# Moving the attention outputs of a head pair one slot back, from the end of a slot to between its two score halves

## The chip, the cores and the metric

The kernel runs on 1 core of a Trainium2 chip. The metric is the device time of one execution in microseconds (us); lower is better. The engines are named as the profile names them: PE (TensorE, matmul), PEld (its weight loads, which overlap PE), DVE (VectorE), ACT (ScalarE), POOL (GpSimd), SP (SyncE, which issues most DMAs). "PSUM" is the memory into which PE writes, in banks of 128 x 512 fp32; eight of them exist here and all eight have names.

## What is computed

A cross-attention layer (16 heads of 64, 256 tokens against 512 context rows, four batches) and after it a small second layer (attention between the 16 head groups of each token, then eight experts mixed by a gate). Cut to the part that the change touches:

```python
lat = layer_norm(latents); ctx = layer_norm(context)
q = (lat @ Wq).reshape(b, n, HEADS, DHEAD).transpose(0, 2, 1, 3)
k, v = jnp.split(ctx @ Wkv, 2, axis=-1)          # heads split in the same way
k = apply_rope(k, cos, sin)
attn = jnp.clip(jnp.einsum('bhnd,bhsd->bhns', q, k) * scale, -11.0, 11.0)
attn = jax.nn.softmax(attn, axis=-1)
out = jnp.einsum('bhns,bhsd->bhnd', attn, v)     # "outputs" of a pair: pv
x = x + (out.transpose(0, 2, 1, 3).reshape(b, n, INNER) @ Wo + bo)
# then the second layer on x (rms norm, q/k/v, att over heads, Wo, gate, 8 experts)
```

## The kernel before

**Slots.** The 16 heads make 8 pairs, and four batches make 32 pairs. Every engine has its own program, written out by hand as a loop over slots from -3 to 32; slot s is about pair s. Order on one engine is fixed by this code, and engines meet through semaphores only. An engine whose next instruction waits does nothing else in the meantime.

**PE in slot s** (lines 739 to 756): the key projection of pair s+3 (`keys`, L517 to L519 on `ctxT,wkA`), the first half of the scores of pair s (`scores`, L579, 12 matmuls), a side step "a", the query projection of pair s+1 (`queries`, L517 to L519 on `latT,wqS`), in even slots the softmax denominators of two pairs (`sums`, L609), the second half of the scores, none to two units of the value projection (`values`, on `wvS`), a side step "b", the outputs of pair s-1 (`times_values`, L593, 16 matmuls in the trace), a side step "c".

**The score loop.** Both halves of the scores go into the same two banks, `sc`. So each half waits for ACT's exponential of the half before it (`s_exp`, lines 572 and 573), which in turn waits for the scores (L805) and writes `e`. POOL then clips `e` (L1515), and `sums` and `times_values` wait for both clips of their pair. `e` has three buffers: the exponential of pair j waits for the outputs of pair j-3 (L807). ACT copies the outputs out of their bank, `pv`, in `attention_copy` (L817).

**Side steps.** What the second layer needs of PE, and the transposes of the next batch, lies in the slots by the tables `POST_STEPS` and `PREP_STEPS` under the places a, b and c. Inside the slots all of them write one and the same bank, `side`, and each waits until the step before it has been read out of the bank by DVE or ACT (line 638, `s_side_free`). In these slots both b and c hold a step:

| slots | step b, who reads it out | step c |
|---|---|---|
| 9, 17, 25 | `norm1`, DVE (L1124) | `norm2` |
| 11, 19 | `ctx_T`, ACT (L839) | `h_T` |
| 18, 26 | `out_proj`, DVE (L1129) | `o_T` |
| 20, 28 | `keyval2`, DVE (L1143) | `h2_T` |
| 22, 30 | `moe0`, ACT (L884, four pieces) | `moe1` |

No other slot has steps at both b and c. `times_values` stood between the two.

**Cover at the end of a slot.** Behind the second half of the scores, slots 5, 8, 13, 16, 21, 24 and 29 hold no values and no side step, only the outputs and the next keys; from slot 29 on there are no next keys either, since pair 32 does not exist.

**DVE in a slot** multiplies the keys by cosine and sine (L1075), splits off the low parts of queries and keys (L1011) and does the work of the second layer on fixed places (`OWN_STEPS`). The value and key projections use two banks, `pj_k`, in turn; each waits until the last use of its bank has been read out by DVE or ACT (`bank_free`). At the end of a batch DVE takes the reciprocals of the sums (L1087) and splits them (`recS`), and `norm0` on PE waits for these.

Of the kernel before, what the change touches and what calls it, by code (L numbers as in the profile page):

```python
# [42 lines left out]
NPAIR = NB * PAIRS  # L43
# [134 lines left out]
def value_units(slot):  # L178


    b, p = divmod(slot, PAIRS)
    if p >= PAIRS - 2 and b + 1 < NB:
        first = 8 * (b + 1) + 2 * (p - (PAIRS - 2))
        return [first, first + 1]
    if 1 <= p <= 4 and 0 <= b < NB:
        return [8 * b + 3 + p]
    return []
# [25 lines left out]
def xattn_ffn(nc, x, ctx, cos, sin, ln_lat_g, ln_lat_b, ln_ctx_g, ln_ctx_b, Wq, Wkv, Wo, bo,  # L213
              gamma1, f_Wq, f_bq, f_Wdown, f_bdown, f_Wup, f_bup, f_Wo, f_bo, gamma2, f_Wg, f_bg, f_We, out):
    es = ExitStack()
    with es:
# [220 lines left out]
        def taken(name, b):  # L437

            k, n = SIDE[name, b]
            return s_side_free[k], n + 1  # L440
# [7 lines left out]
        def query_bank(j):  # L448
            return pj_k[PLACE["queries", j] % 2]
# [64 lines left out]
        def _(pe):  # L514
            def split3(out_ap, w_hi, w_lo, m_hi, m_lo):

                nc.tensor.matmul(out_ap, w_hi, m_hi, start=True, stop=False)  # L517
                nc.tensor.matmul(out_ap, w_hi, m_lo, start=False, stop=False)  # L518
                return nc.tensor.matmul(out_ap, w_lo, m_hi, start=False, stop=True)  # L519

            def bank_free(kind, n):
                if PLACE[kind, n] < 2:
                    return
                kind, n = PROJECTIONS[PLACE[kind, n] - 2]
                if kind == "keys":
                    pe.wait_ge(s_kmul, 2 * n + 2)
                elif kind == "queries":
                    pe.wait_ge(s_qlo, n + 1)
                else:
                    pe.wait_ge(s_v, n + 1)  # L530

            def keys(j):
                b, p = divmod(j, PAIRS)
                cols = slice(128 * p, 128 * p + 128)
                if p == 0:
                    pe.wait_ge(s_ctxT, b + 1)
                if j == 0:
                    pe.wait_ge(s_wk, 1)
                bank_free("keys", j)
                split3(key_bank(j)[:, :], wkA[:, 0, cols], wkA[:, 1, cols], ctxT[:, b % 2, 0, :],  # L540
                       ctxT[:, b % 2, 1, :]).then_inc(s_kproj, 1)

            def queries(j):
                b, p = divmod(j, PAIRS)
                if p == 0:
                    pe.wait_ge(s_latT, b + 1)
                if j == 0:
                    pe.wait_ge(s_wq, 1)
                bank_free("queries", j)
                cols = slice(128 * p, 128 * p + 128)  # L550
                split3(query_bank(j)[:, 0:NT], wqS[:, 0, cols], wqS[:, 1, cols], latT[:, 0, :], latT[:, 1, :]).then_inc(s_qproj, 1)

            def values(n):
                b, unit = divmod(n, 8)
                half, c = divmod(unit, SC)
                if n == 0:
                    pe.wait_ge(s_wv, 1)
                if not value_units_at_first(n):
                    bank_free("values", n)
                rows = slice(128 * c, 128 * c + 128)  # L560
                cols = slice(512 * half, 512 * half + 512)
                split3(value_bank(n)[:, :], ctxT[:, b % 2, 0, rows], ctxT[:, b % 2, 1, rows], wvS[:, 0, cols], wvS[:, 1, cols])\
                    .then_inc(s_vproj, 1)

            def scores(j, half):

                if half == 0:
                    pe.wait_ge(s_klo, j + 1)
                    pe.wait_ge(s_qlo, j + 1)
                if j == 0 and half == 0:  # L570
                    pe.wait_ge(s_v, 2)
                if j or half:
                    pe.wait_ge(s_exp, 2 * j + half)
                for c in range(2):
                    chunk = slice(128 * (2 * half + c), 128 * (2 * half + c) + 128)
                    for k_part, q_part in ((0, 0), (0, 1), (1, 0)):
                        for h in range(2):
                            rows = slice(DH * h, DH * h + DH)
                            last = nc.tensor.matmul(sc[:, h, c * NT:(c + 1) * NT], ks[rows, j % 3, k_part, chunk],  # L579
                                                    qs[rows, j % 2, q_part, :], start=(k_part + q_part == 0),  # L580
                                                    stop=(k_part == 1))
                last.then_inc(s_score, 1)
# [14 lines left out]
            def sums(j):  # L597

                b, p = divmod(j, PAIRS)
                pe.wait_ge(s_clip, 2 * j + 2)  # L600
                if p == 1 and b:
                    pe.wait_ge(s_rec, b)
                if j == 1:
                    pe.wait_ge(s_const, 2)
                    pe.wait_ge(s_v, 4)
                w = sum_rows[:, 24 - 8 * (p // 2):56 - 8 * (p // 2)]
                for c in range(SC):
                    for g in range(4):
                        last = nc.tensor.matmul(sum_bank[32 * g:32 * g + 32, 0:NT], w,  # L609
                                                e[:, (j - 1 + g // 2) % 3, g % 2, c, :],  # L610
                                                start=(p == 1 and c == 0), stop=(p == PAIRS - 1 and c == SC - 1))
                last.then_inc(s_sum, 1)
# [116 lines left out]
            def side_at(slot, pos):  # L729
                step = side_step(slot, pos)  # L730
                if step:
                    side_product(*step)
# [6 lines left out]
            for slot in range(-KEYS_AHEAD, AFTER):  # L739
                if slot + KEYS_AHEAD < NPAIR:  # L740
                    keys(slot + KEYS_AHEAD)
                if 0 <= slot < NPAIR:
                    scores(slot, 0)
                side_at(slot, "a")
                if 0 <= slot + 1 < NPAIR:
                    queries(slot + 1)
                if 2 <= slot <= NPAIR and slot % 2 == 0:
                    sums(slot - 1)
                if 0 <= slot < NPAIR:
                    scores(slot, 1)  # L750
                for n in value_units(slot):
                    values(n)
                side_at(slot, "b")
                if 1 <= slot <= NPAIR:
                    times_values(slot - 1)
                side_at(slot, "c")
            for name, b, k in TAIL_STEPS:
# [11 lines left out]
        def _(act):  # L769
# [18 lines left out]
            def query_hi(j):  # L788
                act.wait_ge(s_qproj, j + 1)
                if j >= 2:  # L790
                    act.wait_ge(s_score, 2 * (j - 2) + 2)
                nc.scalar.activation(qs[:, j % 2, 0, :], query_bank(j)[:, 0:NT], ACT.Copy).then_inc(s_qhi, 1)  # L792
# [10 lines left out]
            def exps(j, half):  # L803

                act.wait_ge(s_score, 2 * j + half + 1)  # L805
                if j >= 3 and half == 0:
                    act.wait_ge(s_pv, j - 2)  # L807
                    act.wait_ge(s_sum, (j - 1) // 2)
                nc.scalar.activation(e[:, j % 3, :, 2 * half:2 * half + 2, :].rearrange("p h c n -> p h (c n)"),  # L809
                                     sc[:, :, :], ACT.Exp, scale=SCALE).then_inc(s_exp, 1)  # L810

            def attention_copy(j):
                act.wait_ge(s_pv, j + 1)
                if j >= PAIRS:

                    act.wait_ge(*taken(f"norm{j % PAIRS // 2}", j // PAIRS - 1))
                nc.scalar.activation(u[:, j % PAIRS, :], pv_bank[:, 0:NT], ACT.Copy).then_inc(s_u, 1)  # L817
# [119 lines left out]
            for slot in range(-KEYS_AHEAD, AFTER):  # L937
                if 0 <= slot < NPAIR:
                    exps(slot, 0)
                side_taken(slot, "a")  # L940
                if 0 <= slot + 1 < NPAIR:
                    query_hi(slot + 1)
                if 0 <= slot < NPAIR:
                    exps(slot, 1)
                for n in value_units(slot):
                    value_copy(n)
                if 0 <= slot + KV_AHEAD < NPAIR:
                    key_hi(slot + KV_AHEAD)
                side_taken(slot, "b")
                if 1 <= slot <= NPAIR:  # L950
                    attention_copy(slot - 1)
                second_layer(slot, "c")
                side_taken(slot, "c")
                second_layer(slot, "end")
                gate_exps(slot)
                if slot == PAIRS - 2:
                    order_columns()
# [684 lines left out]
```

## Time and profile before

| what | value |
|---|---|
| time, median of 3 runs | 344.45 us (344.03 to 344.72) |
| the profiled execution | 343.19 us |
| its span, first to last instruction | 340.3 us |
| granted PE clock, mean | 0.97 of full speed |
| PE busy | 307.5 us (90%) |
| DVE busy | 246.0 us (72%) |
| POOL busy | 202.3 us (59%) |
| ACT busy | 156.5 us (46%) |
| scores L579 busy, 64 halves | 63.5 us |
| outputs L593 busy, 32 pairs | 62.3 us |
| sums L609 busy, 16 times | 30.9 us |

The page gives shares of the whole span. The idle time of PE is spread over a start, a tail and single short waits inside the slots, so the views to read are the table of who waited for whom and the timeline, slot by slot. The start of a matmul group minus the start of the group before it tells how much of PE's time that group took; the durations printed for pipelined matmuls overlap a little, and are not to be added.

### The profile page before, as it was taken

How to read it: one execution, taken by the hardware profiler on the slowest of the kernel's cores; microseconds unless marked ns; L12 is line 12 of the kernel's file. 1: busy time of each engine (PE TensorE's matmuls, PEld its weight loads, DVE VectorE, ACT ScalarE, POOL GpSimd, SP SyncE). 2: the span in 40 equal slices, each digit the busy share in tenths (PEclk: the TensorE clock that was granted, in tenths of full speed). 3: DMA queues.
4: the chain of work that ended last, by engine and by line, in shares of the span. 5: the costliest groups of instructions: out<-in, count | busy, mean ns of one | idle time of the engine just before them, and what ended most of it. 6: DMA issues, size and time to landing. Idle time of an engine off the chain costs nothing.

```text
span 340.3 us, 6782 instructions
## 1 busy us (share of the span) xinstructions
PE 307.5 (90%) x2584; PEld 211.5 (62%) x2584; DVE 246.0 (72%) x470; ACT 156.5 (46%) x291; POOL 202.3 (59%) x206
## 2 busy tenths in 40 slices
PE   6858999999999999997999999997999999889674
PEld 5736666666667666665686666665866645769351
DVE  3956734433893658999938789797375987799977
ACT  2445564566533636644336467753354465020420
POOL 5426654534564659495547593898275937855661
PEclk9797999999999999999999999999999999979985
DMA  8843222111210101101201110111111000000001
GB/s 218 231 134 82 53 47 64 32 33 42 50 34 2 44 22 47 25 24 40 56 0 33 31 41 23 33 34 31 33 31 49 2 0 3 15 2 0 1 0 31
DMA packets 16320, 14.24 MB, mean 42 GB/s; under 512 B 4833, under 2 KB 11809, under 8 KB 16289
## 3 DMA queue, kind: packets, MB, share of 16 engines
q1 hardware_dynamic: 15232, 13.69, 15.4%
q8 instruction: 20, 0.33, 0.4%
q10 hardware_dynamic: 1056, 0.13, 0.2%
q14 instruction: 12, 0.09, 0.1%
HBM read 4.89 MB, written 0.52 MB: 16 GB/s over the span
## 4 chain that ended last, share of the span: by engine, by line
PE 58%; DVE 25%; ACT 7%; POOL 3%; issue 3%; DMA 2%; SPq 0%; ACTq 0%; DVEq 0%; POOLq 0%
PE sc L579 13%; PE pv L593 13%; PE sums L609 7%; PE pj_k L517 5%; ACT e L809 4%; DVE o L1326 3%; PE pj_k L519 3%; PE pj_k L518 3%; PE side L680 3%; DVE ks L1011 2%; PE side L726 2%; PE side L616 2%; DMA sin_in<-in_L_xattn_sin_dram 2%; DVE rec L1087 2%; POOL prod L986 1%
## 5 line engine op out<-in xcount | busy, mean ns | idle before, releaser
L1515 POOL TENSOR_SCALAR e<-e 128x1024 f32<-128x1024 f32 x64 | 68.4, 1069 | 75.6 <-ACT e L809 66.1
L809 ACT ACTIVATE e<-sc 128x1024 f32<-128x1024 f32 x64 | 65.7, 1027 | 76.5 <-PE sc L579 76.5
L579 PE MATMUL sc<-qs,ks 64*128 64x256 f32 x768 | 63.5, 298 | 6.1 <-ACT e L809 4.5
L579 PEld LDWEIGHTS sc<-qs,ks 64*128 64x128 f32 x768 | 50.4, 188 | 28.3 <-issue 17.3
L593 PE MATMUL pv<-e,v 128*64 128x256 f32 x512 | 62.3, 385 | 0.0
L1508 POOL TENSOR_TENSOR krot<-kcos,kswap 128x512 f32<-128x512 f32 x32 | 41.2, 1286 | 11.7 <-DMA kswap<-ksin 9.5
L593 PEld LDWEIGHTS pv<-e,v 128*64 128x64 f32 x512 | 33.9, 136 | 22.4 <-issue 5.6
L1075 DVE TENSOR_TENSOR ksin<-pj_k,sinT 128x512 f32<-128x512 f32 x32 | 22.0, 688 | 34.4 <-PE pj_k L519 30.7
L1011 DVE TENSOR_TENSOR ks<-krot,ks 128x512 fp32r<-128x512 f32 x32 | 33.0, 1030 | 0.0
L609 PE MATMUL sums<-e,sum_rows 128*32 128x256 f32 x512 | 30.9, 382 | 1.0 <-POOL e L1515 1.0
L817 ACT ACTIVATE u<-pv 128x256 f32<-128x256 f32 x32 | 12.3, 385 | 37.7 <-PE pv L593 37.7
L986 POOL TENSOR_TENSOR prod<-q,kv 128x1024 f32<-128x1024 f32 x8 | 19.9, 2496 | 5.6 <-DVE kv L1206 3.5
L1011 DVE TENSOR_TENSOR qs<-pj_k,qs 128x256 fp32r<-128x256 f32 x32 | 13.4, 420 | 13.0 <-ACT qs L792 12.9
L994 POOL TENSOR_TENSOR prod<-att,kv 128x1024 f32<-128x1024 f32 x8 | 19.1, 2398 | 5.9 <-ACT att L903 5.5
L609 PEld LDWEIGHTS sums<-e,sum_rows 128*32 128x32 f32 x512 | 15.0, 109 | 12.1 <-POOL e L1515 2.0
L786 ACT ACTIVATE ks<-krot 128x512 fp32r<-128x512 f32 x32 | 20.1, 627 | 4.9 <-POOL krot L1508 4.9
L1075 DVE TENSOR_TENSOR kcos<-pj_k,cosT 128x512 f32<-128x512 f32 x32 | 21.7, 678 | 0.0
L1326 DVE TENSOR_REDUCE o<-prod 128x64 f32<-128x1024 f32 x16 | 18.8, 1207 | 0.1
L801 ACT ACTIVATE v<-pj_k 128x512 f32<-128x512 f32 x28 | 16.6, 594 | 4.2 <-PE pj_k L519 3.7
L517 PE MATMUL pj_k<-ctxT,wkA 128*128 128x512 f32 x32 | 15.7, 491 | 2.9 <-DVE kcos L1075 2.8
L517 PE MATMUL pj_k<-wvS,ctxT 128*128 128x512 f32 x28 | 13.4, 480 | 3.8 <-DVE kcos L1075 3.8
L1557 POOL TENSOR_TENSOR moe<-moe 128x512 f32<-128x512 f32 (+2 forms) x18 | 15.4, 854 | 1.2
(265 smaller groups left out, 558.9 us busy)
## 6 DMA issues: line engine op xcount, KB each, us to landing
kswap<-ksin SPq DMA_DIRECT2D x128, 64.0 KB, 2.0
ctx_in<-in_ctx_dram SPq DMA_DIRECT2D x4, 256.0 KB, 3.1
prod<-in_L_xattn_Wkv_dram SPq DMA_DIRECT2D x2, 512.0 KB, 6.5
x_in<-in_x_dram SPq DMA_DIRECT2D x1, 512.0 KB, 6.2
prod<-in_L_xattn_Wq_dram SPq DMA_DIRECT2D x1, 512.0 KB, 7.0
wo<-in_L_xattn_Wo_dram SPq DMA_DIRECT2D x1, 512.0 KB, 8.0
fwe<-in_L_ffn_We_dram SPq DMA_DIRECT2D x1, 512.0 KB, 4.0
out_dram<-x_in SPq DMA_DIRECT2D x3, 128.0 KB, 1.8
```

The source lines that it names most:

```text
L517: nc.tensor.matmul(out_ap, w_hi, m_hi, start=True, stop=False)
L579: last = nc.tensor.matmul(sc[:, h, c * NT:(c + 1) * NT], ks[rows, j % 3, k_part, chunk], qs[rows, j % 2, q_part, :], start=(k_part + q_par ...
L593: last = nc.tensor.matmul(pv_bank[DH * h:DH * h + DH, 0:NT], v[:, c, col:col + DH], e[:, j % 3, h, c, :], start=(c == 0), stop=(c == SC - 1))
L609: last = nc.tensor.matmul(sum_bank[32 * g:32 * g + 32, 0:NT], w, e[:, (j - 1 + g // 2) % 3, g % 2, c, :], start=(p == 1 and c == 0), stop= ...
L786: nc.scalar.activation(ks[:, j % 3, 0, :], krot[:, j % 2, :], ACT.Copy).then_inc(s_khi, 1)
L809: nc.scalar.activation(e[:, j % 3, :, 2 * half:2 * half + 2, :].rearrange("p h c n -> p h (c n)"), sc[:, :, :], ACT.Exp, scale=SCALE).then ...
L986: return engine.tensor_tensor(prod[:, t, 1024 * hh:1024 * hh + 1024].rearrange("p (h g d) -> p h g d", h=G // 2, g=G), q_v.unsqueeze(2).to ...
L1011: return nc.vector.tensor_tensor(dst, whole, f(hi), ALU.subtract)
L1075: nc.vector.tensor_tensor(dst[:, j % 2, :], key_bank(j)[:, :], trig[:, :], ALU.mult).then_inc(s_kmul, 1)
L1326: return nc.vector.tensor_reduce(outputs(t)[:, 8 * hh:8 * hh + 8, :], pr, AX, ALU.add)
L1508: nc.gpsimd.tensor_tensor(krot[:, j % 2, :], kcos[:, j % 2, :], kswap[:, j % 2, :], ALU.add)\
L1515: nc.gpsimd.tensor_scalar(a, a, EXP_HIGH, EXP_LOW, ALU.min, ALU.max).then_inc(s_clip, 1)
```

## The change

`times_values` and `attention_copy` take other places in their engines' loops. For slots 2 to 31, PE now runs the outputs of pair s-2 (before: pair s-1) between the queries and the sums, thus between the two score halves, and ACT copies them out ahead of its second exponential. Slot 31 also runs the outputs of pair 30 at the old place, and slot 32 those of pair 31. No instruction is added or removed; side steps, buffers and waits are as they were.

```diff
 (PE)
                 if 0 <= slot + 1 < NPAIR:
                     queries(slot + 1)
+
+                if 2 <= slot < NPAIR:
+                    times_values(slot - 2)
                 if 2 <= slot <= NPAIR and slot % 2 == 0:
                     sums(slot - 1)
...
                 side_at(slot, "b")
-                if 1 <= slot <= NPAIR:
+                if NPAIR - 1 <= slot <= NPAIR:
                     times_values(slot - 1)
 (ACT)
+                if 2 <= slot < NPAIR:
+                    attention_copy(slot - 2)
                 if 0 <= slot < NPAIR:
                     exps(slot, 1)
...
-                if 1 <= slot <= NPAIR:
+                if NPAIR - 1 <= slot <= NPAIR:
                     attention_copy(slot - 1)
```

PE in slot 5 and at the start of slot 6, before (the first L579 is the first half of slot 5, `ctxT,wkA` are keys, `latT,wqS` queries, `pv<-e,v` outputs):

```order
L579 MATMUL sc<-qs,ks 128x256 x12
L517 MATMUL pj_k<-latT,wqS 128x256
L518 MATMUL pj_k<-latT,wqS 128x256
L519 MATMUL pj_k<-latT,wqS 128x256
L579 MATMUL sc<-qs,ks 128x256 x12
L593 MATMUL pv<-e,v 64x256 x8
L517 MATMUL pj_k<-ctxT,wkA 128x512
L518 MATMUL pj_k<-ctxT,wkA 128x512
L519 MATMUL pj_k<-ctxT,wkA 128x512
L579 MATMUL sc<-qs,ks 128x256 x12
```

The same stretch of PE's program with the change:

```order
L579 MATMUL sc<-qs,ks 128x256 x12
L517 MATMUL pj_k<-latT,wqS 128x256
L518 MATMUL pj_k<-latT,wqS 128x256
L519 MATMUL pj_k<-latT,wqS 128x256
L593 MATMUL pv<-e,v 64x256 x8
L579 MATMUL sc<-qs,ks 128x256 x12
L517 MATMUL pj_k<-ctxT,wkA 128x512
L518 MATMUL pj_k<-ctxT,wkA 128x512
L519 MATMUL pj_k<-ctxT,wkA 128x512
L579 MATMUL sc<-qs,ks 128x256 x12
```

The outputs have moved in front of the second score half, and only the keys are left behind it.

PE at the end of slot 11, as a piece of the difference (`ident,ctx_n` is `ctx_T`, step b; `ident,hn` is `h_T`, step c; both write the bank `side`):

```order
 L519 MATMUL pj_k0<-wvS,ctxT 128x512
 L616 MATMUL side<-ident,ctx_n 128x128 x4
-L593 MATMUL pv<-e,v 64x256 x8
 L616 MATMUL side<-ident,hn 128x128 x2
 L517 MATMUL pj_k1<-ctxT,wkA 128x512
```

The two users of the bank `side` now stand directly one behind the other, as in the other ten slots of the table above.

ACT in slot 22, before (`moe<-side,gate` reads `moe0` and then `moe1` out of the bank `side`; `u<-pv` is the copy of outputs, `e<-sc` the exponential):

```order
L809 ACTIVATE e<-sc 128x2x512
L801 ACTIVATE v<-pj_k 128x512 x2
L786 ACTIVATE ks<-krot 128x512
L884 ACTIVATE moe<-side,gate 128x128 x4
L817 ACTIVATE u<-pv 128x256
L884 ACTIVATE moe<-side,gate 128x128 x4
```

With the change (three lines were added above, so L809 is L812 and so on):

```order
L820 ACTIVATE u<-pv 128x256
L812 ACTIVATE e<-sc 128x2x512
L804 ACTIVATE v<-pj_k 128x512 x2
L789 ACTIVATE ks<-krot 128x512
L887 ACTIVATE moe<-side,gate 128x128 x8
```

The copy now stands ahead of the second exponential, and the two read-outs of `side` follow each other.

## Rows read from the trace of the kernel before

**Rows 1.** Waits of PE over the span: total us, times, longest.
```profile
PE pj_k L517 <- DVE kcos L1075: 6.9, 4, 2.8
PE sc L579 <- ACT e L809: 4.5, 9, 0.6
PE sums L609 <- POOL e L1515: 1.0, 1, 1.0
PE side L671 <- DVE recS L1011: 0.6, 1, 0.6
```
**Rows 2.** Timeline of PE, slots 5 and 6: start, us, engine, line, op.
```profile
60.55 0.98 PE L579 MATMUL sc<-qs,ks 64*128 64x256 f32 x12
...
62.65 0.98 PE L579 MATMUL sc<-qs,ks 64*128 64x256 f32 x12 [0.57 <-ACT e L809]
63.55 1.95 PE L593 MATMUL pv<-e,v 128*64 128x256 f32 x16
65.43 0.50 PE L517 MATMUL pj_k<-ctxT,wkA 128*128 128x512 f32 x1
...
66.33 0.98 PE L579 MATMUL sc<-qs,ks 64*128 64x256 f32 x12
```
**Rows 3.** Chain that ended last, in order of time: one step, between them.
```profile
61.57 1.03 ACT e L809
```
**Rows 4.** Timeline of PE, slot 19: end of the queries, second score half.
```profile
178.90 0.28 PE L519 MATMUL pj_k<-latT,wqS 128*128 128x256 f32 x1
179.30 0.98 PE L579 MATMUL sc<-qs,ks 64*128 64x256 f32 x12
```
**Rows 5.** Timeline of PE and DVE, slot 9: behind norm1.
```profile
93.82 1.95 PE L593 MATMUL pv<-e,v 128*64 128x256 f32 x16
...
94.00 0.69 DVE L1124 TENSOR_TENSOR on<-u,side 128x512 f32<-128x512 f32 x1 [0.82 <-PE side L672]
```
**Rows 6.** Timeline of PE and DVE, slot 18: behind out_proj.
```profile
174.26 1.95 PE L593 MATMUL pv<-e,v 128*64 128x256 f32 x16
...
174.44 0.42 DVE L1129 TENSOR_TENSOR x_in<-side,x_in 128x256 f32<-128x256 f32 x1 [3.57 <-PE side L680]
```
**Rows 7.** Timeline of PE and DVE, slot 20: behind keyval2.
```profile
192.02 1.95 PE L593 MATMUL pv<-e,v 128*64 128x256 f32 x16
...
192.20 0.69 DVE L1143 TENSOR_TENSOR kv<-side,fbkv 128x512 f32<-128x512 f32 x1 [2.06 <-PE side L706]
```
**Rows 8.** Timeline of PE and ACT, slot 11: behind ctx_T.
```profile
113.35 1.95 PE L593 MATMUL pv<-e,v 128*64 128x256 f32 x16
...
114.04 0.78 ACT L839 ACTIVATE ctxT_f<-side,vec 128x512 f32<-128x512 f32 x1
```
**Rows 9.** Timeline of PE and ACT, slot 22: behind moe0.
```profile
207.58 1.95 PE L593 MATMUL pv<-e,v 128*64 128x256 f32 x16
...
207.84 1.14 ACT L884 ACTIVATE moe<-side,gate 128x128 f32<-128x128 f32 x4
```
**Rows 10.** Timeline of DVE: last waits before its two full stretches, and recS.
```profile
128.82 0.42 DVE L1011 TENSOR_TENSOR qs<-pj_k,qs 128x256 fp32r<-128x256 f32 x1 [0.55 <-ACT qs L792]
135.46 0.42 DVE L1011 TENSOR_TENSOR qs<-pj_k,qs 128x256 fp32r<-128x256 f32 x1 [0.91 <-ACT qs L792]
...
155.55 0.42 DVE L1011 TENSOR_TENSOR recS<-rec,recS 128x256 fp32r<-128x256 f32 x1
...
214.74 0.42 DVE L1011 TENSOR_TENSOR qs<-pj_k,qs 128x256 fp32r<-128x256 f32 x1 [2.06 <-ACT qs L792]
```
**Rows 11.** Timeline of PE where those two stretches end, slots 17 and 25.
```profile
160.50 0.50 PE L517 MATMUL pj_k<-wvS,ctxT 128*128 128x512 f32 x1 [2.04 <-DVE kcos L1075]
...
232.09 0.50 PE L517 MATMUL pj_k<-wvS,ctxT 128*128 128x512 f32 x1 [1.77 <-DVE kcos L1075]
```
**Rows 12.** Busy time by stretch (PE, PEld, DVE, ACT, POOL, then PEclk, DMA).
```profile
228.00:234.00 6.00, 3.88 (x32) 3.15 (x34) 5.97 (x10) 3.12 (x5) 5.68 (x7) 1.00 0.11 28
```
**Rows 13.** Timeline of PE, slot 30: sums.
```profile
272.67 1.93 PE L609 MATMUL sums<-e,sum_rows 128*32 128x256 f32 x32 [1.00 <-POOL e L1515]
```

## The prediction

> **What bounds the kernel now.** I read the waits of PE first, then its timeline slot by slot, then the timelines of DVE, ACT and POOL at the places where PE waits. PE is the busiest engine, and inside the slots it waits little: for exponentials, for DVE's key products, once for POOL's clip, once for the reciprocals [rows 1]. So the time of the slots is nearly PE's own work, and the change can gain no more than these waits, while each new hole in PE's row is paid at once. The exception is two stretches in which DVE never waits, from 135.5 to 160.4 and from 214.7 to 232.0 us [rows 10]; at the end of each PE waits for DVE [rows 11]. There DVE sets the time, and PE has 2.04 and 1.77 us to spare.
>
> The score loop has a floor. From one score half to the next at least 2.10 us pass (60.55 to 62.65), since the exponential runs from 61.57 to 62.60 and PE goes on 0.05 us later [rows 2, 3]. PE's work between two halves is free of waits only if half plus work last 2.10 us.
>
> **What the change removes: the waits between the halves.** In slot 5 PE has only the queries there and idles 0.57 us; a group normally starts 0.07 us before the printed end of the one before (63.55 + 1.95 = 65.50 against 65.43), so the hole is 0.64 us [rows 2]. The outputs take 1.88 us (63.55 to 65.43 [rows 2]) and now fill it. Slots 3, 5, 7, 11, 13 and 15 are alike: 6 x 0.64 = 3.8 us. In slots 9, 17, 19, 21, 27 and 29 a side step fills most of the hole; the rest is 179.30 - 178.90 - 0.28 + 0.07 = 0.19 us [rows 4], six times 1.1 us. In slot 30 the sums wait 1.00 us for POOL's clip [rows 13], and the outputs now stand in front of them: 1.0 us. In slot 31, where the outputs of pair 29 fill the hole, I take 0.2 us by the same row [rows 4]. Sum: 6.1 us. ACT's copy ahead of the second exponential costs nothing: ACT waits there for the second score half anyway, which PE runs after those outputs.
>
> **What it adds, first: short ends of slots.** Behind the second score half slot 5 now has the keys alone. From 62.65 to 66.33 PE took 3.68 us; without the outputs 1.80, and the floor is 2.10 [rows 2]: 0.30 us lost. Slots 5, 8, 13, 16, 21 and 24 are so: 1.8 us. In slot 29 there are no keys either: one half of 0.90 us (3.68 - 1.88 - 0.90, the keys being 65.43 to 66.33 [rows 2]) against 2.10, 1.2 us lost. Sum: 3.0 us.
>
> **Second: the bank `side`.** In eleven slots the outputs stood between steps b and c, and these share one bank, so c may start only when b has been read out. The outputs hid that. Now c comes to the head of PE's queue when the outputs used to start, and waits for the reader's end plus 0.05 us [rows 3]. Behind it in PE's queue stand the next keys and the next scores, so the whole slot moves.
> - `norm2` behind `norm1`: DVE reads 94.00 to 94.69, PE could go on at 93.82: 0.92 us [rows 5]; slots 9, 17, 25: 2.8 us.
> - `o_T` behind `out_proj`: 174.86 + 0.05 - 174.26 = 0.65 us [rows 6], slots 18, 26: 1.3 us.
> - `h2_T` behind `keyval2`: 192.89 + 0.05 - 192.02 = 0.92 us [rows 7], slots 20, 28: 1.8 us.
> - `h_T` behind `ctx_T`: ACT comes to it late, behind an exponential, a value copy and a key copy, 114.82 + 0.05 - 113.35 = 1.52 us [rows 8], slots 11, 19: 3.0 us.
> - `moe1` behind `moe0`: four pieces on ACT, 208.98 + 0.05 - 207.58 = 1.45 us [rows 9], slots 22, 30: 2.9 us.
>
> Sum: 11.8 us. The reading engine's place in its own order is the same behind the second score half, so the lag carries over. The bounds: nothing, if the read-out were long over when PE arrives, which rows 5 to 9 contradict, and 1.88 us each, the whole cover.
>
> The Trainium skill, "Perfetto Trace Analysis", section Optimizing Tensor Performance, Matmuls, says that independent matmul groups should rotate through different PSUM banks, so that one is read out while the next runs. By that rule this change is the wrong way round: two groups of one bank come to stand together. The rows show the mechanism and its size, and the sum above goes by them alone.
>
> **Third: DVE's stretches.** On PE alone the balance would be 11.8 + 3.0 - 6.1 = +8.7 us. But part of it falls where DVE sets the time, so I go through in order.
> - Up to slot 12: lost 0.30 (slot 8), 0.30 (slot 5), 0.92, 1.52; gained four times 0.64 (3, 5, 7, 11) and 0.19 (9). Balance +0.3 us.
> - First stretch. DVE waited 0.55 and 0.91 us for query copies just before it [rows 10]. Queries now reach ACT earlier than DVE wants them, as the outputs no longer stand ahead of keys and queries at a slot's start, so these 1.46 us go. DVE ends 1.46 - 0.3 = 1.1 us earlier than before, and PE, which had 2.04 us to spare, follows: -1.1 us at the values of slot 17. One new wait lies inside: `norm0` of slot 17 needs `recS`, ready at 155.97 before [rows 10], and PE now arrives about 0.9 us ahead of it; that fits into what is left of the 2.04 us.
> - Slots 17 to 23: +0.92, +0.65, +1.52 - 0.19, +0.92, -0.19 + 0.30, +1.45 = +5.4: balance +4.3 us. DVE's second stretch starts from a query copy [rows 10] which is now issued 1.88 us earlier within the slots: +2.4 us. It ends +2.4 us late. PE's own path would be there at +4.2 and still had 1.77 us to spare [rows 11], so both meet at +2.4 us.
> - From slot 25 on: +0.92, +0.65 - 0.19, +0.92, -0.19 + 1.2, -1.0, +1.45, -0.2 = +3.6: balance +6.0 us.
>
> Behind slot 31 nothing changes place: DVE waits for the last sums, and the tail starts later by all of it. The clock gives no further term: in a stretch with a PE wait of 1.77 us it was granted in full [rows 12], and the new waits are shorter. (On this, the Trainium skill, "TensorE: Matmul & The Clock Gate", section HAM oscillation, holds that waits between bursts can put the clock down by half; by it the eleven new holes might cost more, and the rows show no such fall.)
>
> So the profiled execution of 343.19 us (span 340.3) would become 349.2 us. It was 1.3 us quicker than the median of the runs, 344.45 us; on that the forecast is **350.4 us**, 1.7% slower.
>
> **The rivals.**
> - *DVE hides nothing.* If DVE's stretches begin later than I say (its waits before them stay, and `recS` comes late because the sums now stand 1.88 us later in slots 8, 16 and 24), PE's balance of 8.7 us stands in full, and some 1 us more if `norm0` waits in slots 9 and 25 as well: 353 to 354 us. For it: the rows show the sparing only at two places. Against: those are 3.8 us of real idle time of PE.
> - *The bank waits are half.* If ACT and DVE, relieved of the outputs' copy at the slot's end and of waiting for it, reach the read-outs sooner, the 11.8 us become some 6, and the time is +6.0 - 5.9 = 344.5 us: no change. Only the five slots read by ACT have a queue that could shrink; DVE sat waiting in rows 5 to 7, so it has nothing to gain.
> - *Faster.* The copy of the outputs is gone from ACT's row at the end of a slot, and queries and keys reach DVE 1.88 us earlier within each slot; if by that step b is read out before PE comes to c in all eleven slots, no bank wait is left, and what remains is 344.45 + 3.0 - 6.1 = 341.4 us. It decides at bank waits of about 5.8 us in all, half a microsecond each, below which the change gains; rows 5 to 9 all stand above that.
> - *The change does not do what it says*: the order of PE in slots 5 and 11 shows that it does, and I give it nothing.
>
> **How the numbers follow.** Forecast (348 to 352) 0.65, DVE hides nothing (352 to 355) 0.17, half the bank waits (343.8 to 348) 0.12, faster 0.06. The range, 346.5 to 353.8, leaves some 0.1 out below and 0.07 above. A difference of 0.2%, 0.7 us, is about what a measurement of this kernel can tell from none: slower takes the forecast, the first rival and half of the second (0.88), same most of the rest of the second (0.05), faster the third and a hundredth of the second (0.07).
>
> **What would show each step.** In the trace of the changed kernel the waits of the scores for the exponential should vanish between the halves and come back at 0.2 to 0.3 us at the ends of slots 5, 8, 13, 16, 21, 24, and at 1.1 us in slot 29. PE should wait for DVE's L1124, L1129 and L1143 (the lines of before; all three are three lines further down now) 0.6 to 0.9 us seven times, and for ACT's read-outs of `ctx_T` and `moe0` 1.4 us four times. The wait for key products in slot 17 should fall from 2.0 to about 0.5 us, and the one in slot 25 to nearly nothing. The prediction is wrong if the waits on `side` sum to less than 6 us, or if the two waits for key products keep their size while the rest comes as said.

## The result, and the profile after

| | before | after |
|---|---|---|
| time, median | 344.24 us (342.98 to 344.72, 4 runs) | 351.75 us (351.48 to 352.14, 4 runs) |
| ratio, 95% interval | | 1.0216 [1.0173, 1.0258] |
| profiled execution, its span | 343.19, 340.3 us | 351.48, 349.7 us |
| granted PE clock, mean | 0.970 | 0.966 |

The change makes the kernel 2.2% slower, 7.5 us between the medians. The forecast was 350.4 us, 6.0 us over the 344.45 us that were known when it was made; the range, 346.5 to 353.8, held the time.

The page of the changed kernel: its span, the busy time of the engines, and the groups of the score loop with DVE's key split (count | busy us, mean ns of one | idle before them and what ended it):
```profile
span 349.7 us, 6782 instructions
...
PE 307.7 (88%) x2584; PEld 211.9 (61%) x2584; DVE 251.8 (72%) x470; ACT 156.4 (45%) x291; POOL 202.5 (58%) x206
...
L579 PE MATMUL sc<-qs,ks 64*128 64x256 f32 x768 | 63.8, 299 | 4.7 <-ACT e L812 3.5
L593 PE MATMUL pv<-e,v 128*64 128x256 f32 x512 | 62.3, 385 | 0.0
L1016 DVE TENSOR_TENSOR ks<-krot,ks 128x512 fp32r<-128x512 f32 x32 | 35.8, 1119 | 0.0
```
PE is as busy as before (307.7 against 307.5 us) in a span 9.4 us longer: the added time is waiting. Who makes it wait stands in the waits of PE in the changed kernel, cut to the score loop, from the second half of the scores of slot 1 (32.65 us) to that of slot 31 (290.28). Columns as in [rows 1]: total us, times, longest:
```profile
PE side L671 <- DVE on L1129: 3.1, 3, 1.4
PE side L726 <- ACT moe L887: 3.0, 3, 1.4
PE sc L579 <- ACT e L812: 3.0, 6, 1.2
PE side L616 <- ACT ctxT_f L842: 2.9, 2, 1.5
PE side L671 <- DVE recS L1016: 2.1, 2, 1.6
PE side L616 <- DVE kv L1148: 1.7, 2, 0.9
PE side L616 <- DVE x_in L1134: 1.2, 2, 0.6
PE pj_k L517 <- DVE kcos L1080: 1.1, 3, 0.6
PE sc L579 <- DVE ks L1016: 1.1, 1, 1.1
```
Five of these rows, on `side` for `on`, `moe`, `ctxT_f`, `kv` and `x_in`, are steps c that wait for the read-out of their step b. They sum to 11.9 us; 0.3 us of it, a third wait for `moe` (slot 31), was there before. The wait of the sums for POOL [rows 1, 13] is gone.

PE's timeline in slot 5 of the changed kernel (start, us, engine, line) shows both sides of the move, and answers [rows 2]:
```profile
58.25 1.95 PE L593 MATMUL pv<-e,v 128*64 128x256 f32 x16
60.12 0.97 PE L579 MATMUL sc<-qs,ks 64*128 64x256 f32 x12
...
62.30 0.98 PE L579 MATMUL sc<-qs,ks 64*128 64x256 f32 x12 [0.31 <-ACT e L812]
```
The second half of the scores (60.12) follows the outputs without a wait, where 0.57 us stood before. At the slot's end only the keys are left, and the next scores wait 0.31 us. Slot 11, PE and then ACT, answers [rows 8]:
```profile
111.08 0.60 PE L616 MATMUL side<-ident,ctx_n 128*128 128x128 f32 x4
113.13 0.44 PE L616 MATMUL side<-ident,hn 128*128 128x128 f32 x2 [1.45 <-ACT ctxT_f L842]
```
```profile
111.30 0.59 ACT L804 ACTIVATE v<-pj_k 128x512 f32<-128x512 f32 x1
111.78 0.63 ACT L789 ACTIVATE ks<-krot 128x512 fp32r<-128x512 f32 x1
112.30 0.78 ACT L842 ACTIVATE ctxT_f<-side,vec 128x512 f32<-128x512 f32 x1
```
`ctx_T` leaves PE at about 111.6; ACT comes to its read-out at 112.30, behind a value copy and a key copy, and ends it at 113.08. `h_T` starts 0.05 us later. All of it was predicted; 1.45 against 1.52 us is a matter of counting, since the view takes a wait from the printed end of the group before (111.08 + 0.60 = 111.68) and the forecast from 0.07 us earlier.

### The profile page after: what moved, and what is told of

It reads as the page before. It is cut to its first block, busy times and chain, and to the rows that moved or that the text cites. A ratio compares the mean times of both kernels' runs of the same rounds, so it can differ in the third digit from the quotient of the medians.

```text
span 349.7 us, 6782 instructions
## 1 busy us (share of the span) xinstructions
PE 307.7 (88%) x2584; PEld 211.9 (61%) x2584; DVE 251.8 (72%) x470; ACT 156.4 (45%) x291; POOL 202.5 (58%) x206
## 4 chain that ended last, share of the span: by engine, by line
PE 58%; DVE 28%; ACT 5%; issue 5%; DMA 2%; POOL 1%; SPq 0%; DVEq 0%; ACTq 0%; POOLq 0%
PE pv L593 13%; PE sc L579 12%; PE sums L609 7%; PE pj_k L517 5%; PE side L680 3%; PE pj_k L519 3%; PE pj_k L518 3%; DVE ks L1016 3%; DVE o L1331 2%; PE side L726 2%; ACT e L812 2%; ACT moe L887 2%; DVE ksin L1080 2%; DVE rec L1092 1%; DVE kcos L1080 1%
## 5 line engine op out<-in xcount | busy, mean ns | idle before, releaser
L1520 POOL TENSOR_SCALAR e<-e 128x1024 f32<-128x1024 f32 x64 | 69.1, 1079 | 85.6 <-ACT e L812 81.3
L812 ACT ACTIVATE e<-sc 128x1024 f32<-128x1024 f32 x64 | 65.6, 1026 | 71.8 <-PE sc L579 71.8
L579 PEld LDWEIGHTS sc<-qs,ks 64*128 64x128 f32 x768 | 50.7, 189 | 29.5 <-issue 24.0
L579 PE MATMUL sc<-qs,ks 64*128 64x256 f32 x768 | 63.8, 299 | 4.7 <-ACT e L812 3.5
L1016 DVE TENSOR_TENSOR ks<-krot,ks 128x512 fp32r<-128x512 f32 x32 | 35.8, 1119 | 0.0
L991 POOL TENSOR_TENSOR prod<-q,kv 128x1024 f32<-128x1024 f32 x8 | 19.6, 2454 | 6.4 <-DVE kv L1211 4.3
L1016 DVE TENSOR_TENSOR qs<-pj_k,qs 128x256 fp32r<-128x256 f32 x32 | 13.4, 418 | 11.8 <-ACT qs L795 11.7
```

The costliest lines, as they stand in the source:

```text
L991: return engine.tensor_tensor(prod[:, t, 1024 * hh:1024 * hh + 1024].rearrange("p (h g d) -> p h g d", h=G // 2, g=G), q_v.unsqueeze(2).to ...
L1016: return nc.vector.tensor_tensor(dst, whole, f(hi), ALU.subtract)
L1520: nc.gpsimd.tensor_scalar(a, a, EXP_HIGH, EXP_LOW, ALU.min, ALU.max).then_inc(s_clip, 1)
```

## The experiments

The spans differ by more than the loop does, since start and tail of this program vary by a microsecond: the changed kernel, run a second time, gave a loop of 257.69 us where it had 257.63, while its tail was 58.05 us where it had been 59.42. So beside the ratios, each of which is to the kernel before as it ran in the same row of runs, I compare the loop, scores of slot 1 to scores of slot 31 as above, and the waits that the view lists inside it. The column of the exponential also has the wait just ahead of the loop's first scores (0.56 us in the first two rows, 0.24 in the last):

| kernel | loop | on the bank of step c | exponential | key split `ks` | `recS` | `kcos` | other | all listed |
|---|---|---|---|---|---|---|---|---|
| before | 248.9 | 0.3 | 4.0 | - | 0.6 | 3.8 | 1.0 | 9.7 |
| after | 257.6 | 11.9 | 3.0 | 1.1 | 2.1 | 1.1 | 0.4 | 19.6 |
| outputs late in the eleven slots | 250.6 | 0.3 | 3.9 | - | 2.1 | 4.6 | 0.4 | 11.3 |
| step c behind the next keys | 256.6 | 6.3 | 3.0 | 1.8 | 2.1 | 1.1 | 1.5 | 15.8 |
| step c in another bank | 247.4 | 1.1 | 1.8 | 3.5 | 2.2 | 1.1 | 0.8 | 10.5 |
| bank and places | 247.3 | 1.1 | 1.0 | 3.1 | 1.6 | 1.1 | 0.5 | 8.4 |
| bank, places and product | 244.4 | 1.1 | 0.9 | 1.8 | 1.6 | 1.1 | 0.4 | 6.8 |

From before to after the listed waits grow by 9.9 us and the loop by 8.8; the difference is the six holes of 0.19 us [rows 4], 1.1 us, which are too short to be listed. Three of the loops hold something more that no wait shows: PE's granted clock fell to half for some 3 us (outputs late: from about 160.5 to 163.5 us; step c behind the next keys: 270 to 273; bank and places: 200 to 203), which took about 1.6 us of each. In the loops of the other four it stood at full speed.

My theory: the bank waits cost the time. Rivals: the lag of a slot in itself; the new place between the halves in any slot; the order against the sums; the copy ahead of the exponential. Unless it is said otherwise, edits are made on the changed kernel.

**Where the outputs stand.** Three kernels take the outputs of pair s-2 between the halves in some slots, and put them back between steps b and c in the others:
```diff
-                if 2 <= slot < NPAIR:
+                if 2 <= slot < NPAIR and between(slot):
                     times_values(slot - 2)
...
                 side_at(slot, "b")
+                if 2 <= slot < NPAIR and not between(slot):
+                    times_values(slot - 2)
```
(ACT's copy likewise.) In the first `between` is false in the eleven slots that hold both b and c, in the second it is true in those alone, in the third it is always false, which leaves the lag by itself.

> The changed kernel, but in the eleven slots with side steps at both b and c (9, 11, 17 to 20, 22, 25, 26, 28, 30) the outputs of pair s-2 and their copy stand between b and c again. Theory S (the bank side): the changed kernel's PE waits there, 3.1 + 1.2 + 1.7 for DVE and 2.9 + 2.7 for ACT, 11.6 us, go; the holes between the score halves that the outputs filled in these slots come back (0.64 in slot 11, 0.2 in five others, the sums' wait for the clip in slot 30, 1.0), some 2.6 us: 351.75 - 11.6 + 2.6 = 342.8 us, or up to 345 where DVE is in the lead. Rival D (the loss comes from DVE's two full stretches and from the outputs being one slot late, which stays here): 349 to 352.

> The opposite half: outputs of pair s-2 everywhere, but between the score halves only in the eleven slots with side steps at both b and c, and at the end of the slot in all others. Theory S: 11.6 us of waits against 2.6 us of holes filled, less what DVE's stretches hide (up to 3.8): 344.2 + 9 - 3.8 to + 0 = 349.5 to 353. Rival D: most of the moves are undone, so 344 to 346.

> Outputs of pair s-2 and their copy at the old place, at the end of the slot, in every slot: the one-slot lag alone. Theory S: neither the holes nor the side waits are touched, 344.2 within 1 us. Rival D: the lag itself moves DVE's and POOL's work against each other and costs several us: 347 or more.

Measured: with the outputs late in the eleven slots 344.35 us, ratio to before 1.0000 [0.9967, 1.0032]; between the halves in the eleven alone 351.68 us, 1.0228 [1.0158, 1.0299]; the lag alone 343.88 us, 0.9992 [0.9953, 1.0032]. The whole loss sits in the eleven slots, and neither the lag nor the place between the halves costs anything in the other nineteen. It gains nothing there either: five of the six large holes are filled, 3.2 us, but the short ends of seven slots give them back, and DVE makes PE wait longer, `kcos` 4.6 against 3.8 us and `recS` 2.1 against 0.6 in the table. (The loops of the other two kernels hold one group of outputs fewer than these and are not compared.) PE's waits in slot 17 of the first of these kernels, at `norm0` and at the values, and the outputs behind them:
```profile
154.48 0.36 PE L675 MATMUL side<-recS,spread 128*128 128x256 f32 x1 [1.57 <-DVE recS L1024]
...
158.85 0.50 PE L521 MATMUL pj_k<-wvS,ctxT 128*128 128x512 f32 x1 [2.41 <-DVE kcos L1088]
...
160.22 3.47 PE L597 MATMUL pv<-e,v 128*64 128x256 f32 x16
```
PE waits 1.57 + 2.41 us for DVE within five microseconds, where it had waited 2.04 [rows 11]. The outputs behind take 3.40 us up to the next group (163.62) and not 1.88: the granted clock was 0.74 from 160 to 161 us and 0.50 from 161 to 163. So of the 1.7 us by which this loop is longer than that of before, 1.6 are the clock.

**Step c in another bank.** The sharper test keeps the place between the halves in all slots and takes away only what makes c wait. Step c of the eleven slots writes `pv`, which is free there, since its outputs were copied out in the middle of the slot; the next outputs wait until c has been read out:
```diff
+C_SLOT = {side_step(slot, "c"): slot for slot in range(NPAIR) if side_step(slot, "b") and side_step(slot, "c")}
...
+    in_slots = {step: 6 for step in C_SLOT}
...
+                read_out = sum(slot < j + 2 for slot in C_SLOT.values())
+                if read_out:
+                    pe.wait_ge(s_side_free[6], read_out)
...
+                elif (name, b) in C_SLOT:
+                    pe.wait_ge(s_u, C_SLOT[name, b] - 1)
```

> The changed kernel; in the eleven slots with side steps at both b and c, step c writes the bank of the outputs (pv), which is free there since the outputs of pair s-2 were copied out before, and no longer the bank side. Theory S: all eleven waits (11.6 us in the changed kernel's profile) go and the filled holes stay; where DVE is in the lead some of it is not seen: 351.75 - 11.6 = 340.2 us at best, 343 if DVE's stretches end as in the changed kernel. Rival D (the outputs between the halves cost by what they do to DVE and POOL, the bank is a symptom): 347 or more.

Measured: 342.64 us, 0.9964 [0.9934, 0.9995], and a loop 10.2 us shorter than that of the changed kernel. This shows the cause. Slot 11 on PE, where 1.45 us stood between the two steps:
```profile
112.33 0.60 PE L624 MATMUL side<-ident,ctx_n 128*128 128x128 f32 x4
112.77 0.38 PE L624 MATMUL pv<-ident,hn 128*128 128x128 f32 x2
```
The price of using `pv` is small: the read-out of `norm2` now holds up the outputs of slots 10 and 18, 1.1 us in all. DVE's key split has become the largest wait in the loop (3.5 us). Without its bank waits the move is no loss, and by a third of a per cent a gain, whose interval ends at 0.9995.

**Step c behind the next keys.** Keys of 0.90 us put between b and c should cover half of each bank wait:
```diff
                     keys(slot + KEYS_AHEAD)
+                side_at(slot - 1, "c")
                 if 0 <= slot < NPAIR:
                     scores(slot, 0)
```

> The changed kernel with one thing more: PE runs side step c behind the next slot's keys (0.90 us of work) and not ahead of them. Theory S: each wait on side shrinks by 0.90, so those behind norm1, out_proj and keyval2 go or stay under 0.5 us, those behind ctx_T and moe0 (slot 22) fall to about 0.5, and slot 30, which has no keys behind it, keeps its 1.3: about 8.5 us less than the changed kernel, 343 to 345 us. Rival D: PE's order there does not matter, 350 to 352.

Measured: 350.66 us, 1.0198 [1.0140, 1.0257], a miss: hardly better than the change itself, and inside what the rival had. The waits of the loop fall by 3.8 us, the loop by 1.0. Three rows of its PE timeline (slots 10, 22, and the keys behind slot 27) show where cover went, and a fourth (slot 29) where time went without a wait:
```profile
95.83 0.39 PE L671 MATMUL side<-recS,spread 128*128 128x256 f32 x1 [0.78 <-DVE on L1130]
...
202.50 0.97 PE L579 MATMUL sc<-qs,ks 64*128 64x256 f32 x12 [1.78 <-DVE ks L1017]
...
256.77 0.50 PE L517 MATMUL pj_k<-ctxT,wkA 128*128 128x512 f32 x1 [0.73 <-DVE qs L1017]
...
270.89 3.06 PE L593 MATMUL pv<-e,v 128*64 128x256 f32 x16
```
Step c moves 0.90 us nearer to step a of the next slot, and in slots 10 and 18 that one (`norm3`) waits on the same bank instead (0.78 and 0.79 us). The first scores of slot 22 wait 1.78 us for DVE where they waited 1.12, and the keys behind slot 27 wait for DVE's part of the queries in their bank. From slot 29 on there are no keys, so the steps c of slots 28 and 30 keep their waits of 0.85 and 1.31. With one bank in the row b, c, next a, the cover given to one pair was taken from the next in those slots. Of the 2.8 us of this loop that no listed wait shows, 1.6 us are the clock: it was granted at 0.50 from 270 to 273 us, and slot 29 took 5.39 us from its first to its second scores where the changed kernel took 3.79. The other 1.2 us are open. So the clock hides part of what the later place gives, but even without it the loop would be 2.6 us shorter and not 8.5.

**The order against the sums.** `sums` ahead of `times_values(slot - 2)`.

> The changed kernel with the sums ahead of the outputs in even slots. The sums then end 1.88 us earlier, as before the change. If the waits of norm0 for the reciprocals (2.1 us in two slots) and DVE's 1.0 us wait for the sums in slot 24 come from the outputs standing ahead of the sums, they go, and the sums of slot 30 wait for POOL's clip again (1.0 us): 350 to 351 us. If DVE's own queue sets them, nothing but the 1.0 us changes: 351.7 to 352.8.

Measured: 354.12 us, 1.0287 [1.0227, 1.0347], above both expectations, the loop 0.8 us longer than the changed kernel's. The waits of `norm0` in slots 9 (0.38) and 25 (0.52) do vanish, as the rival in the prediction had it, that in slot 17 only falls from 1.58 to 1.24, but the sums then wait for POOL's clip 2.3 us in all:
```profile
134.20 1.07 PE L609 MATMUL sums<-e,sum_rows 128*32 128x256 f32 x16 [1.48 <-POOL e L1520]
```
So in the loop the outputs ahead of the sums are the better order, and it was no cause of the loss.

**ACT's copy.** `attention_copy(slot - 2)` back at its old place behind step b.

> The changed kernel with ACT's copy of the outputs back behind the second exponential, at its old place behind step b. The prediction held that the copy ahead of the exponential costs nothing: 351.75 within 0.7 us, and by the same reasoning the late copy costs nothing either. If ACT's copy delays the exponential on which the next scores wait (0.08 us more at each short end), this comes out 0.5 us faster.

Measured: 354.69 us, 1.0296 [1.0245, 1.0346], 2.2 us above the expectation; the loop is the same as the changed kernel's to 0.1 us, and each of the short ends in slots 5, 8, 13 and 24 still takes 2.18 or 2.19 us, so the copy is not what makes them longer than 2.10. One new wait stands behind it, before the last outputs, since the copy of pair 29 now comes behind the last exponential:
```profile
294.83 1.95 PE L593 MATMUL pv<-e,v 128*64 128x256 f32 x16 [1.49 <-ACT u L820]
```
The copy ahead of the exponential costs nothing in the loop, as predicted, and saves 1.5 us at its end; the rest of the longer time is open.

**The product beside the key split.** In the changed kernel the first scores of slot 22 wait 1.12 us for `ks`, a wait that before did not have. DVE and POOL of the changed kernel in slot 21, each in order of time:
```profile
201.11 2.73 DVE L1016 TENSOR_TENSOR ks<-krot,ks 128x512 fp32r<-128x512 f32 x1
203.76 2.34 DVE L1178 TENSOR_REDUCE own_bank<-prod 128x128 f32<-128x1024 f32 x2
```
```profile
199.78 1.04 POOL L1520 TENSOR_SCALAR e<-e 128x1024 f32<-128x1024 f32 x1
200.91 2.38 POOL L991 TENSOR_TENSOR prod<-q,kv 128x1024 f32<-128x1024 f32 x1
```
The split is an instruction of 0.68 us that takes 2.73 here, and ends at 203.84, 0.55 us behind POOL's product (203.29). To test it, the product goes half a slot later:
```diff
-    "products_1b": [(5, 0)],
+    "products_1b": [(5, 1)],
```

> The changed kernel with POOL's second product of the second layer (products_1b) behind the clip of the second half and not ahead of it, in slots 13, 21 and 29. If DVE's key split of 2.73 us in slot 21 (0.7 alone) is slowed by POOL's product beside it, it falls below 1.4 us, the scores of slot 22 no longer wait 1.1 us for it, and the time is 350 to 351 us. If the split is slow for another reason, 351.7 within 0.7.

Measured: 353.13 us, 1.0272 [1.0209, 1.0334], no gain by the ratio and 2.1 us above what the theory had; but in the trace the loop is 0.9 us shorter and the wait for `ks` is gone. DVE and POOL there:
```profile
202.28 0.68 DVE L1016 TENSOR_TENSOR ks<-krot,ks 128x512 fp32r<-128x512 f32 x1
```
```profile
200.96 1.04 POOL L1520 TENSOR_SCALAR e<-e 128x1024 f32<-128x1024 f32 x1
204.17 1.04 POOL L1520 TENSOR_SCALAR e<-e 128x1024 f32<-128x1024 f32 x1 [2.17 <-DMA kswap<-ksin]
```
With nothing of POOL beside it the split takes 0.68 us. The mechanism is shown; that it moves the time of this kernel is not shown by this run.

**The three together.** Step c in `pv`, and the outputs at the slot's end in slots 8, 16, 21, 24 and 29, so that those ends do not run short; with the product at its place and with the product moved. The changed kernel ran again beside them.

> The same without POOL's product moved. Theory (prices add): the 2.0 us wait for DVE's key split of 2.7 us may stay in slot 22 or change with the place of the outputs in slot 21: 338.5 to 341. Rival (DVE hides it): 341 to 342.6, and then no difference from the run with the product moved.

> Step c of the eleven slots in the bank pv (as in the run before), POOL's second product behind the second clip, and the outputs at the end of the slot in slots 8, 16, 21, 24 and 29, where they leave the next scores to wait for the exponential. Theory: each price seen so far is its own and they add: against the run with the bank alone (342.6 us), 0.3 us less at each of slots 8, 16, 24 and 21, 1.0 less in slot 29, 0.4 to 0.6 less at norm0 of slots 9 and 25 since the sums end earlier, and the 2.0 us wait of slot 22's scores for DVE's key split falls to the 0.3 us of the exponential: 337.5 to 339.5 us, 1.5% faster than before. Rival: DVE is in the lead by now and hides it: 341 to 342.6.

> The changed kernel itself, on the chip of the two kernels beside it. 351.8 us and 1.022 of before if chips do not differ; the three variants of it that were run on another chip came out at 1.027 to 1.030, and if that is the chip and not the edits, it may show here or not. Its slots, from the second score half of slot 1 to that of slot 31, should take 257.6 us as in its first profile.

Measured: without the product's move 341.27 us, 0.9906 [0.9871, 0.9941]; with it 338.78 us, 0.9849 [0.9807, 0.9891], faster than both kernels. The changed kernel again: 351.46 us, 1.0213 [1.0162, 1.0263]. It repeats the first result. The three edits above stand at 1.027 to 1.030, though their loops differ from the changed kernel's by less than 1 us; whether that is the edits or the row of runs in which they ran is open. The chip, which the expectation suspects, was the same one in both rows of runs. The time without the product's move lies 0.3 us above what was expected and within what its rival gave (341 to 342.6), but the rival also had no difference between the two, and there is one: 2.5 us between the medians, though the intervals just overlap. The scores of slot 22, and then DVE's key split, with all three:
```profile
198.09 0.98 PE L588 MATMUL sc<-qs,ks 64*128 64x256 f32 x12 [0.51 <-DVE ks L1034]
```
```profile
196.66 1.38 DVE L1034 TENSOR_TENSOR ks<-krot,ks 128x512 fp32r<-128x512 f32 x1
```
and without the product's move (with the outputs that follow):
```profile
199.37 1.13 PE L588 MATMUL sc<-qs,ks 64*128 64x256 f32 x12 [1.83 <-DVE ks L1034]
...
201.69 2.79 PE L605 MATMUL pv<-e,v 128*64 128x256 f32 x16
```
```profile
196.62 2.69 DVE L1034 TENSOR_TENSOR ks<-krot,ks 128x512 fp32r<-128x512 f32 x1
```
The split starts at the same time in both and lasts 1.3 us less; PE waits 1.3 us less. The loops differ by 2.9 us, and 1.5 us of the rest is the clock again: without the product's move it was granted at 0.50 from 200 to 203 us, behind the wait of 1.83 us, and slot 22 took 6.91 us between its scores and not 5.37. Over its twelve executions the five with a mean clock of 0.974 or more took 338.35 to 340.82 us, the seven with 0.965 or less 341.12 to 342.73. So a part of the difference between the medians is the clock, and whether the longer wait brings that fall about is not shown: in the kernel with the other bank alone PE waits 2.04 us at the same place, and the clock stayed full.

## Why the prediction was right, and where it was not

**Holes between the halves: right.** They are gone in all slots named, with the wait of the sums in slot 30.

**Short ends of slots: right, 0.08 us too small each.** The floor was taken as 2.10 us and is 2.18 (60.12 to 62.30 above): 0.38 to 0.40 instead of 0.30 us in slots 5, 8, 13 and 24. In slots 16 and 21 a wait for DVE stands in its place, and they lose 0.49 and 1.20 us. In slot 29 PE waits 1.21 us against 1.2.

**Bank waits: right.** Forecast 11.8 us; the rows give 11.9 with the 0.3 that was there, so 11.6. One by one: `norm2` 0.85, 1.39 and 0.85 (0.92), `h_T` 1.45 and 1.47 (1.52), `o_T` 0.59 twice (0.65), `h2_T` 0.85 twice (0.92), `moe1` 1.38 and 1.31 (1.45). All but one are 0.05 to 0.14 us under the forecast, about 0.07 of it for where a wait is counted from; in slot 17 DVE came late. The reading engine's place had not moved, so the distance from its end to PE's arrival, read in rows 5 to 9, carried over. That the waits are the loss is shown by the other bank. This case agrees with the rule of the Trainium skill, "Perfetto Trace Analysis", section Optimizing Tensor Performance, Matmuls, that independent groups should rotate through banks: with the rotation 0.9964, without it 1.0216. The rival that halves the waits, and the faster one that needed them below 5.8 us, fall with this.

**DVE's first stretch: wrong.** I took its two query waits, 0.55 and 0.91 us [rows 10], as waits for PE that vanish, and forecast the values of slot 17 at -1.1 us. They came at +0.1. The 0.55 went, but the key split behind it took 0.34 of it back: 1.02 us before (from 129.16), 1.36 after (from 128.29), each ending about 0.54 us behind a clip of POOL (see the last section). The 0.91 is still there to the digit; DVE, then ACT of the changed kernel:
```profile
132.40 0.43 DVE L1182 TENSOR_TENSOR own_bank<-own_bank,amax 128x256 f32<-128x256 f32 x1
...
134.93 0.42 DVE L1016 TENSOR_TENSOR qs<-pj_k,qs 128x256 fp32r<-128x256 f32 x1 [0.91 <-ACT qs L795]
```
```profile
132.87 0.37 ACT L906 ACTIVATE own_bank<-own_bank 128x256 f32<-128x256 f32 x1 [2.61 <-DVE own_bank L1182]
133.15 1.02 ACT L812 ACTIVATE e<-sc 128x1024 f32<-128x1024 f32 x1
134.05 0.57 ACT L855 ACTIVATE latT_f<-side,vec 128x256 f32<-128x256 f32 x1
134.50 0.39 ACT L795 ACTIVATE qs<-pj_k 128x256 fp32r<-128x256 f32 x1
```
It is a loop of DVE and ACT in which nobody waits for PE: ACT is held 2.61 us (before: 1.55) by its exponential of DVE's own product, then works off a queue of three, and the query copy comes last. The step that failed is "queries now reach ACT earlier, so these 1.46 us go": I read the releaser of the wait, ACT's `qs`, and not what ACT had been waiting for.

**The second stretch: wrong.** Forecast +2.4 us at the values of slot 25, measured +5.4. The 2.06 us before it [rows 10] stayed as well, for the same sort of reason (ACT's four pieces of `moe`). And PE itself came later than I had it. Its waits from slot 22 to slot 25 in the changed kernel:
```profile
203.89 0.98 PE L579 MATMUL sc<-qs,ks 64*128 64x256 f32 x12 [1.12 <-DVE ks L1016]
...
214.07 1.13 PE L726 MATMUL side<-fwe,h2T 128*128 128x512 f32 x2 [1.38 <-ACT moe L887]
...
233.25 0.36 PE L671 MATMUL side<-recS,spread 128*128 128x256 f32 x1 [0.52 <-DVE recS L1016]
```
The forecast had left out the short end of slot 24: with it PE's own path stood at 0.3 us more, +2.8 by the prediction's own terms. Beyond the +2.4: 1.2 from the first stretch, 0.5 for `norm2` in slot 17, 0.9 for `ks` in slot 22 (slot 21's end loses 1.20 and not 0.30), 0.4 for slot 24's end, which makes the 3.0 us; the four bank waits between and the `norm0` wait of slot 25, 0.52 us where it had been 0.61, add nothing. PE then starts the values of slot 25 without a wait, and the last key product of DVE ended just before:
```profile
237.02 0.50 PE L517 MATMUL pj_k<-wvS,ctxT 128*128 128x512 f32 x1
```
```profile
236.26 0.67 DVE L1080 TENSOR_TENSOR kcos<-pj_k,cosT 128x512 f32<-128x512 f32 x1
```
The two arrive within 0.1 us of each other (236.93 and 237.02). So DVE did hide what PE had to spare here, all of the 1.77 us.

**From slot 25 on: right.** Forecast +3.6, measured +3.4.

So the loop grew by 8.8 us and not by 6.0. That this is nearly PE's own balance of +8.7, the number of the first rival (DVE hides nothing), makes that rival right at one of the two places only. At slot 17 PE waits 1.58 us for `recS` and 0.56 at the values, 2.14 in place of 2.04: DVE sets that point as before and gave nothing back. At slot 25 the 1.77 us were hidden, and about as much came on top that neither had: 0.9 us for `ks`, 0.5 for `norm2`. In the terms of the table, the bank waits brought 11.6 us, `recS` 1.5, `ks` 1.1 and `norm0` of slot 9 (under "other") 0.4; `kcos` gave back 2.7, the exponential and the sums 1.0 each, the six unlisted holes 1.1. That the time came out at 351.75, within 1.4 us of the forecast, is part mechanism and part luck: the profiled execution rose by 8.3 us, the medians by 7.5.

The clock gave no term in the loop here, as forecast: it was granted in full through both loops. But the reason given, that the new waits are shorter than one behind which the clock stayed, does not hold in general. In the traces above it fell to half behind waits of 2.41 and 1.83 us, and once where the longest wait of the 25 us before was 0.85; it stayed behind 2.04 us in two kernels. The length of a wait does not tell it.

## What to carry to other kernels

Where a group of matmuls is moved, look at which bank its two neighbours use: what stood between them was also the cover of a read-out, and its price can be read before the change as the reader's end less PE's arrival (here right to 0.14 us in ten of eleven places). If it goes, give the second neighbour another bank rather than a later place. And follow a wait of a second engine one step further back than the releaser that the view names, before you count it as slack that earlier work will use up.

## What the runs showed of the hardware

I had not expected how exactly DVE's key split waits for POOL. In six places its end lies 0.54 to 0.55 us behind the end of the POOL instruction beside which it started, be it a clip or a product:

| place | POOL instruction, end | key split: start, us, end | behind |
|---|---|---|---|
| before, slot 21 | clip, 198.13 | 197.72, 0.95, 198.67 | 0.54 |
| before, slot 15 | clip, 144.17 | 143.87, 0.84, 144.71 | 0.54 |
| after, slot 21 | product, 203.29 | 201.11, 2.73, 203.84 | 0.55 |
| after, slot 15 | product, 145.03 | 143.40, 2.18, 145.58 | 0.55 |
| bank and places, slot 21 | product, 198.77 | 196.62, 2.69, 199.31 | 0.54 |
| all three, slot 21 | clip, 197.50 | 196.66, 1.38, 198.04 | 0.54 |

The other traces say the same: of some 290 key splits in all thirteen that start beside a row of POOL with more than 0.15 us to run, all but 16 end 0.52 to 0.57 us behind it. The 16 are rows of several POOL instructions in one and a small one of 128x2 elements (37.62 to 38.32 us in the changed kernel), beside which the split takes its 0.68 us. So the two do not share, DVE is held until POOL is done, and it is the end of POOL's instruction that counts: moving the product away put a clip of 1.1 us in its place. POOL pays as well: its product, 2.38 us alone, takes 2.69 or 2.70 when the key split is running as it starts. DVE's sum over products, TENSOR_REDUCE with one input, does not feel it: 2.34 us beside a POOL product (198.59, before) and beside a clip (203.76, after). The Trainium skill, "SBUF — State Buffer", section SBUF: two separate sides, says of the port pair that DVE and GpSimd have in common that whoever starts first holds it for the whole instruction, and that a DVE operation with two SBUF inputs takes part in this, against a GpSimd operation that reads SBUF; every row of the table agrees. The rows do not show why the split ends 0.54 us behind POOL when it takes 0.68 alone. So a small shift in one engine's row can make this DVE instruction four times as long (0.68 to 2.73 us), and a prediction that moves such instructions can be wrong by up to those 2 us at each of them.
